# Two-layer transformer on one core: shared-expert weights loaded during the second attention, expert totals summed in PSUM by TensorE, and results finished for two chunks at once

## The reference

```python
scores = sigmoid(xf @ gate_w + bias)
top_scores, top_idx = top_k(scores, 2)           # weights of the two chosen experts
up = einsum('th,ehi->tei', xf, up_w) + up_b
eo = einsum('tei,eih->teh', gelu(up), down_w) + down_b
combined = einsum('teh,te->th', eo * 0.1, w)      # routed rows, two per token
shared = (gelu(xf @ sw_up + sb_up) @ sw_down + sb_down) * 0.1
out = shared + combined
out = out / (max(abs(out), axis=-1) + 1e-06)
return x + attention + out
```

## Time and profile before

| what | us |
|---|---|
| runs, median (lowest to highest, 3 runs) | 1303.87 (1302.80 to 1305.22) |
| profiled execution, its time | 1305.71 |
| profiled execution, span of the core | 1304.0 |
| mean granted TensorE clock, of full speed | 0.926 |
| TensorE busy | 1127.9 (86%) |
| VectorE busy | 971.5 (75%) |
| ScalarE busy | 740.4 (57%) |
| GpSimd busy | 509.9 (39%) |

### The profile page before, as it was taken

How to read it: one execution, slowest core, us unless ns; L and a number is a source line. 1 busy time by engine, 2 the same in 40 slices (tenths; PEclk the granted TensorE clock), 3 DMA queues, 4 the chain that set the end, 5 groups by cost and what they waited for, 6 DMA issues and landing times. The chain is left out here.

```text
span 1304.0 us, 22545 instructions
## 1 busy us (share of the span) xinstructions
PE 1127.9 (86%) x7455; PEld 619.1 (47%) x7458; DVE 971.5 (75%) x2126; ACT 740.4 (57%) x1143; POOL 509.9 (39%) x778
## 2 busy tenths in 40 slices
PE   4768879999999999999996755799999969999983
PEld 2436653444333434443433433444444438888862
DVE  8979978788888888888842533777777646777788
ACT  3657531666666656665664322166656557777762
POOL 6002220323233323332212526176666661566663
PEclk9889995999999999999987776599999989999997
DMA  4322970013121213120000121012222153678452
GB/s 130 97 79 68 129 85 18 26 38 126 34 75 50 91 35 99 38 94 27 2 2 1 54 76 44 23 48 64 58 64 63 38 178 110 189 235 241 152 130 65
DMA packets 94975, 103.51 MB, mean 79 GB/s; under 512 B 17217, under 2 KB 72838, under 8 KB 94864
## 3 DMA queue, kind: packets, MB, share of 16 engines
q1 hardware_dynamic: 88928, 93.09, 26.4%
q0 software_dynamic: 4992, 8.48, 1.9%
q10 hardware_dynamic: 944, 0.54, 0.2%
HBM read 64.67 MB, written 38.43 MB: 79 GB/s over the span
## 5 line engine op out<-in xcount | busy, mean ns | idle before, releaser
L1112 ACT ACTIVATE a_probs<-a_pst 128x1024 f32<-128x1024 f32 (+4 forms) x544 | 414.4, 813 | 284.5 <-PE a_pst L1060 284.0
L1136 DVE TENSOR_REDUCE a_tops<-a_ps 128x1 f32<-128x512 f32 (+9 forms) x624 | 341.4, 590 | 92.4 <-PE a_ps L1030 84.1
L976 POOL TENSOR_SCALAR_AFFINE_SELECT a_probs<-a_probs 128x256 f32<-128x256 f32 (+3 forms) x384 | 179.8, 480 | 387.3 <-ACT a_probs L1112 382.6
L1030 PE MATMUL a_ps<-kp,qp 96*128 96x512 bf16 (+9 forms) x1280 | 292.8, 307 | 0.8 <-DVE a_tops L1136 0.4
L1060 PE MATMUL a_pst<-qp,kp 99*128 99x512 bf16 (+4 forms) x1088 | 260.7, 332 | 22.6 <-DMA qp<-a_top_rows 18.9
L1079 PE MATMUL a_po<-a_probs,vh 128*32 128x512 f32 (+4 forms) x2176 | 233.1, 501 | 2.0 <-POOL a_probs L976 1.9
L1136 DVE TENSOR_REDUCE a_tops_lead<-a_ps 128x1 f32<-128x512 f32 x256 | 161.8, 683 | 5.7 <-PE a_ps L1030 5.4
L1027 PE MATMUL a_ps<-mask_s,identb 128*128 128x128 bf16 (+8 forms) x624 | 144.3, 234 | 7.0 <-PEq L1220 4.5
L1030 PEld LDWEIGHTS a_ps<-kp,qp 96*128 96x128 bf16 x1280 | 111.9, 101 | 79.1 <-DVE a_tops_lead L1136 15.3
L1060 PEld LDWEIGHTS a_pst<-qp,kp 99*128 99x128 bf16 (+1 forms) x1088 | 92.1, 100 | 120.1 <-ACT a_probs L1112 48.4
L1678 POOL DMA_INDIRECT chosen_rows<-e_slot_y,e_slot_x x92 | 93.4, 1015 | 87.9 <-DVE e_slot_y L1866 60.3
(11 more groups left out here) (269 smaller groups left out, 1715.7 us busy)
## 6 DMA issues: line engine op xcount, KB each, us to landing
e_slot_w<-weight_parts SPq DMA_DIRECT2D x23, 1024.0 KB
weight_parts<-a_cut SPq DMA_DIRECT2D x18, 512.0 KB, 3.1
qp<-q_parts SPq DMA_DIRECT2D x64, 96.0 KB
slot_rows<-empty_row SPq DMA_DIRECT2D x4, 1495.0 KB, 27.3
e_slot_x<-slot_rows SPq DMA_DIRECT2D x23, 260.0 KB, 5.4
a_raw<-in_wraw SPq DMA_DIRECT2D x18, 256.0 KB, 3.7
qp<-q_parts SPq DMA_DIRECT2D x64, 64.0 KB
q_parts<-o SPq DMA_DIRECT2D x24, 128.0 KB
```

The source lines that it names most:

```text
L976: pool.affine_select(out=seen, in_=seen, compare_op=ALU.is_ge, fill=0.0, base=m0, pattern=[[0, 2], [1, mw]], channel_multiplier=-1 if laye ...
L1030: last = pe.matmul(bank[:, i * room:i * room + w], sb["qp"][slot][0:KROWS, j, f["qt"] * P:(f["qt"] + 1) * P], sb["kp"][slot][0:KROWS, j // ...
L1112: act.activation(probs[local % RING][0:st["rows"], 2 * part:2 * part + 2, st["off"]:CHUNK], p_st[part][0:st["rows"], :, st["off"]:CHUNK], ...
L1136: dve.tensor_reduce(out, scores, AX.X, ALU.max).then_inc(s["banks_read"], 1)
```

## The change

Four things are changed.

1. The shared expert's weights and bias (`shared_w`, `shared_b`) get buffers that live through the whole program. Their three DMAs are issued by SP at the end of attention 1's list (`load_shared`) and no longer at the head of `experts`.
2. GpSimd's 16 adds of the totals are gone. The total of a chunk is now summed in a PSUM bank by TensorE: for chunks 2 to 7 the turned sums are written there (`turn_total`), for chunks 0 and 1 the kept rows in `e_acc` are multiplied by the identity, and then the two routed rows are added by two products with the identity as the stationary operand (`add_rows`, 128x512 in fp32). `e_acc` holds only two chunks, and ScalarE copies only those.
3. The banks `e_pt`, `e_pa`, `e_px`, `e_py` are used in turn, in the order `FINAL` of the chunks; `bank_free` is what TensorE waits for before it writes one again. `TURN_AT` and `ADD_AT` say at which step a turn or an add stands; the adds of the last three chunks stand behind the last step.
4. VectorE finishes two chunks at once: two reductions, three small instructions on 8 columns, eight result instructions. Results go to `big` (the whole input of the stage, no longer read by then), so there is no wait for a store. Two pair finishes stand at steps 121 and 124, two behind the last step. SP loads the routed rows in the order of `FINAL`.

```diff
+def load_shared(sp, io, sb, dram):
+    for i in range(2):
+        sp.wait_ge(sb["counts"]["experts"][f"cut_stored{i}"], START + 16 * CUTS // 2)
+    shared_in = sb["landed"]["shared"]
+    sp.dma_start(sb["shared_b"][:, :], io["wbias"][EXPERTS, :, :]).then_inc(shared_in[0], 16)
+    for c in range(2):
+        sp.dma_start(sb["shared_w"][:, 2 * c:2 * c + 2, :].rearrange("p a h -> p (a h)").bitcast(F32),
+                     dram["weights"][2 * EXPERTS + c, :, :]).then_inc(shared_in[c], 16)
...
+            if layer == 1:
+                load_shared(sp, io, sb, dram)
...
+        p_total = [p_t, p_a, p_x, p_y]
-        FINISH_AT = [HT * (JOBS - 2 + i // 2) + 2 * (i % 2) + 1 for i in range(4)]
-        LATE_FINISHED = len(FINISH_AT)
+        FINAL = [2, 3, 0, 4, 1, 5, 6, 7]
+        FINISH_AT = {HT * (JOBS - 1) + 1: 0, HT * JOBS: 1}
+        TURN_AT = {HT * (EARLY + n + SLOT_TILES + 2): EARLY + n for n in range(3)}
+        TURN_AT.update({HT * JOBS: 5, HT * JOBS + 2: 6, HT * (JOBS + 1): 7})
+        ADD_AT = {HT * (JOBS - 2) + 1: 0, HT * (JOBS - 2) + 3: 1, HT * (JOBS - 1) + 1: 2, HT * (JOBS - 1) + 3: 3,
+                  HT * JOBS + 1: 4}
...
-            for n in range(CHUNKS):
-                pool.wait_ge(chosen_in[n // 2], 2 * 16 * TOPK)
-                tiles = slice(n * CT, (n + 1) * CT)
-                pool.tensor_tensor(picked[0][:, tiles, :], picked[0][:, tiles, :], picked[1][:, tiles, :], ALU.add)\
-                    .then_inc(s["pairs_added"], 1)
-                pool.wait_ge(s["pairs_added"], START + n + 1)
-                pool.wait_ge(s["rows_done"], START + shared_job(n) + 1)
-                pool.tensor_tensor(acc[:, tiles, :], acc[:, tiles, :], picked[0][:, tiles, :], ALU.add)\
-                    .then_inc(s["totals_added"], 1)
...
+            def turn_total(n):
+                at, j = FINAL.index(n), shared_job(n)
+                pe.wait_ge(s["sums_read"], START + j + 1)
+                bank_free(at)
+                for t in range(CT):
+                    last = pe.matmul(p_total[at % 4][:, t * P:(t + 1) * P], sums[j % 2][:, t * P:(t + 1) * P],
+                                     sb["ident"][:, :], start=t == 0, stop=False, is_transpose=True,
+                                     skip_group_check=True)
+                last.then_inc(s["y_turned"], 1)
+
+            def bank_free(at):
+                if at == 0:
+                    pe.wait_ge(s["ot_copied"], START + CHUNKS)
+                elif at == 1:
+                    pe.wait_ge(s["x_added"], START + CHUNKS)
+                elif at == 2:
+                    pe.wait_ge(s["x_tail"], START + EARLY + SLOT_TILES)
+                elif at == 3:
+                    pe.wait_ge(s["rows_done"], START + EARLY + SLOT_TILES)
+                else:
+                    pe.wait_ge(s["res_ready"], START + CT * (at - 3))
+
+            def add_rows(at):
+                n = FINAL[at]
+                tiles = slice(n * CT, (n + 1) * CT)
+                whole = p_total[at % 4][:, :].rearrange("p (t e) -> p t e", e=E)
+                if n < EARLY:
+                    bank_free(at)
+                    pe.wait_ge(s["rows_done"], START + n + 1)
+                    pe.matmul(whole, sb["ident"][:, :], acc[:, tiles, :], start=True, stop=False, skip_group_check=True)
+                if at % 2 == 0:
+                    pe.wait_ge(chosen_in[at // 2], 2 * 16 * TOPK)
+                for i in range(TOPK):
+                    last = pe.matmul(whole, sb["ident"][:, :], picked[i][:, tiles, :], start=False, stop=i == TOPK - 1,
+                                     skip_group_check=True)
+                last.then_inc(s["totals_added"], 1)
...
-                if k == 0 and j >= 2:
+                if k == 0 and 2 <= j < 2 + EARLY + SLOT_TILES:
                     turn_y(j - 2)
+                if m in TURN_AT:
+                    turn_total(TURN_AT[m])
+                if m in ADD_AT:
+                    add_rows(ADD_AT[m])
...
             run(step)
+            for at in range(len(ADD_AT), CHUNKS):
+                add_rows(at)
...
+            def finish(pair):
+                step, base = s["res_steps"], RES * pair
+                total = [p_total[at % 4][:, :].rearrange("p (t e) -> p t e", e=E) for at in (2 * pair, 2 * pair + 1)]
+                for i in range(2):
+                    dve.wait_ge(s["totals_added"], START + 2 * pair + i + 1)
+                    dve.tensor_reduce(top[:, i * CT:(i + 1) * CT], total[i], AX.X, ALU.max, apply_absolute_value=True)\
+                        .then_inc(step, 1)
...
+                for i in range(2):
+                    n = FINAL[2 * pair + i]
+                    for t in range(CT):
+                        dve.scalar_tensor_tensor(res[:, n * CT + t, :], total[i][:, t, :], inv[:, i * CT + t:i * CT + t + 1],
+                                                 X[:, n * CT + t, :], ALU.mult, ALU.add).then_inc(s["res_ready"], 1)
```

More of the change, by code:

```diff
@@ L1574, in experts @@
         sums = [tmp(f"sums{i}", [P, CHUNK]) for i in range(2)]
[L1575 removed]
+        acc = tmp("acc", [P, EARLY * CT, E])
         o_t = tmp("o_t", [P, CHUNK])
[L1577 to L1578 removed]
+        top, inv = tmp("top", [P, 2 * CT]), tmp("inv", [P, 2 * CT])
         p_up = [bank(f"pup{i}") for i in range(UR)]
@@ L1818, in step @@
                     act.activation(o_t[:, :], p_t[:, :], ACT.Copy).then_inc(s["ot_copied"], 1)
-                if k == 0 and j >= 2 and shared_chunk(j - 2) is not None:
+                if k == 0 and 2 <= j < 2 + EARLY:
                     keep_rows(j - 2)
@@ L1905, in step @@
                 if m in FINISH_AT:
-                    finish(FINISH_AT.index(m))
+                    finish(FINISH_AT[m])
             stage_x(0)
             run(step)
-            for n in range(LATE_FINISHED, CHUNKS):
-                finish(n)
+            for pair in range(len(FINISH_AT), CHUNKS // 2):
+                finish(pair)
 def build(nc, io, out):
```

47 lines of the change are left out of this document (16 added, 31 removed).

## The result

The changed kernel takes 1290.66 us (median of 4 runs, 1289.20 to 1291.62), the kernel before, run beside it on the same chip, 1304.55 (1302.80 to 1306.50). The ratio is 0.9892, 95% interval 0.9874 to 0.9911: faster by 13.9 us, where 7.2 were forecast. The direction was right, the size too small by almost half.

A forecast was written before the change was run, and what follows sets the result against it. Bound by TensorE's own sum up to 1265, then by VectorE slowed beside GpSimd's adds, finally by VectorE's finishes. Start 0.6 plus end 6.6 gave 7.2 us off 1303.87: 1296.7, range 1293.8 to 1300.8.

The forecast's parts named there:

- 0.6 + 6.6 = 7.2 us: Whole forecast gain: 0.6 us at the experts' start plus 6.6 at the end, nothing elsewhere.
- recorded range: Forecast bounds for the changed kernel's time: 1293.8 us to 1300.8 us.
- start (to job 1): Head of experts' stage: early shared-weight load starts TensorE 0.55 us sooner; 0.6 taken as gain to job 1.
- the second of the two readings: Experts' start: VectorE stays tied to the ends of GpSimd's adds, gain between 0 and 1.4 us, a step.
- GpSimd's adds go: Late experts' stage: without 16 adds, VectorE subtractions return to 0.69 us; 4.65 us stall and slow clock vanish.
- TensorE's adds: Totals on TensorE: each fp32 identity product costs 0.86 us; 0.97 upper bound at full clock, 1.86 at the slow one.
- rival A: TensorE pays more: adds at 0.97 us plus small gaps; gain 4 to 5, about 1299.5 us; chance 0.14.
- Waits for routed rows and banks: From step 117: routed rows land and pair finishes free banks before TensorE needs them; no stall.
- Rival B: From step 117: late routed rows idle TensorE, which then runs at slow clock; about 1311.5 us; chance 0.04.
- the slack from step 117: First four routed-row loads landed by 1259.50, needed at 1262.6: 3.1 us of slack.
- The end: Last down to turn 1.17 us, pair finish 4.12, store tail 2.81; VectorE ends at 1294.6, not 1301.19: 6.6 saved.
- Rival D: More gain: start's step falls well (1.4 us), fewer small gaps at end; gain 9, about 1295 us; chance 0.08.

The follow-up runs named there:

- e1: Kernel before with 32 unused bytes per partition after the last kept buffer, moving every attention buffer by 32 bytes: 1297.35 us, ratio 0.995.
- e14: Changed kernel with 32 unused bytes ahead of the routed weights (e_slot_w), in the experts' stage alone: 1293.30 us, ratio 0.9906.
- e5: Kernel before with only the early load of the shared weights into kept buffers, totals and finishes as before: 1297.18 us, ratio 0.9948.
- e9: e8 with GpSimd's bias adds also spread over the first eight jobs (all but the first hunk): 1285.30 us, ratio 0.9848.
- e13: e9 with 32 unused bytes ahead of all the experts' temporaries: 1284.95 us, ratio 0.9839.
- e16: e9 with 96 unused bytes ahead of all the experts' temporaries: 1286.47 us, ratio 0.9845.
- e12: Kernel before with 32 unused bytes ahead of the routed weights (e_slot_w), in the experts' stage alone: 1303.71 us, ratio 0.9994.
- e15: Kernel before with 96 unused bytes ahead of the routed weights, in the experts' stage alone: 1310.52 us, ratio 1.0017, times widely spread.
- e17: Kernel before with 224 unused bytes ahead of the routed weights, in the experts' stage alone: 1302.52 us, ratio 0.9972.
- e18: Kernel before with 2016 unused bytes ahead of the routed weights, in the experts' stage alone: 1304.72 us, ratio 0.9988.
- e3: Kernel before with the attention's operands (v1, qp, kp, vh) moved by 32 bytes and the temporaries by 64: 1297.15 us, ratio 0.9951.
- e7: Changed kernel with 16 GpSimd adds put back on two buffers nobody else reads: 1301.33 us, ratio 0.9971.
- e4: Kernel before with only the attentions' temporaries moved by 32 bytes, operands where they were: 1299.61 us, ratio 0.9976.
- e10: Kernel before with 64 unused bytes after the last kept buffer: 1301.87 us, ratio 0.9994.
- e2: Changed kernel with 32 unused bytes, attention buffers placed as in the kernel before modulo 64: 1293.96 us, ratio 0.9923.
- e6: Changed kernel without the early load: shared weights loaded at the head of the experts' stage into the same kept buffers: 1289.06 us, ratio 0.9877.
- e11: Kernel before with 96 unused bytes after the last kept buffer: 1301.48 us, ratio 0.9971.
- e8: Changed kernel with the adds of chunks 5 and 6 placed ahead of the last turn: 1289.35 us, ratio 0.9895.

## Why the prediction was wrong, by its steps

The step that failed is a term that is not written down: the sum "0.6 + 6.6 = 7.2 us" put the place of the buffers, which the kept shared buffers move, at nothing without a reason, in the attentions and in the routed jobs alike. The runs showed 6.6 us there (e1) and 2.3 (e14). Eight other profiled kernels have the changed kernel's placement in the attentions (e5 to e9, e13, e14, e16), four others that of before (e12, e15, e17, e18), and the two groups keep apart: attention 0 and 1 together took 735.4 to 739.2 us in the changed kernel and its eight, and 741.6 to 746.3 in before and its four. The means are 7.0 us apart (737.3 and 744.3), so some 2.5 of the 9.5 us in the first table are the spread of single executions. The runs e1 and e3 make it a cause: 6.6 and 6.8 us by 32 bytes. The routed jobs' 2.2 us are the second part that was counted at nothing; e14 gives 2.3 for it. That the recorded range missed is due to these two; the two terms that were priced, 7.2 us, measured 6.5.

| term | predicted, us | measured in the profiles, us |
|---|---|---|
| start (to job 1) | 0.6 | 0.15 |
| routed jobs | 0 | 2.2 |
| end | 6.6 | 6.4 |
| experts' stage in all | 7.2 | 8.7 |
| attentions and what lies between | 0 | 8.4 (9.5 less 1.1); 6.6 in the medians of e1 |

*Start.* The first product came 0.45 us sooner on the stage's clock, near the 0.55; job 1 only 0.15. The ends of GpSimd's adds set when VectorE gets on, as the second of the two readings in the prediction had it. The Trainium skill (SBUF — State Buffer, Who interferes with whom) gives that reading: a lock for a whole instruction, so a step and not a rate. The traces agree: a cast takes 1.53 beside the adds and 0.43 in e9 without them, and an earlier start bought no earlier end. The 0.6 taken was the wrong choice of the two.

*GpSimd's adds go.* Right: subtractions 0.69 up to the end, no stall, clock 1.00. e7 gives the other side, 10.7 us for having them beside TensorE's adds.

*TensorE's adds.* 0.86 us, as taken from the one row of another stage; rival A falls: the range was open to a smaller gain by it, not to the larger one that came.

*Waits for routed rows and banks.* None; TensorE's only wait after job 1 is the 0.34 us before its last turn. Rival B did not occur, and the slack from step 117 held.

*The end.* Last down to turn 1.17 forecast, 1.18 measured; a pair 4.12 and 4.12; the tail 2.81 and 2.8. From job 29 on 6.4 in place of 6.6. The count of TensorE's end took 0.229 us for each product, from the shared jobs of before; they took 0.233 after, and for the 51 products from step 117 on that is 0.2 us (an estimate from these two paces), which fits the difference.

*Rival D* names 9 us, and the stage gained 8.7 by luck for it, but its reasons (a good step at the start, fewer gaps at the end) are not what happened.

**What stays open.** Why the last packet's wait depends on the address, and by which rule (e4 and e10 fit no simple one). Why the changed kernel loses only 3.3 us to the 32 bytes that give the old one 6.6 (e2). Whether a distance of 192 bytes is fast or in between, and why the shared jobs are slower than the routed ones at the same distance. The sum of the parts found, 6.6 by e1 and 8.7 in the experts' stage, is 15.3 us, 1.4 more than the medians' 13.9; nothing here says where the rest lies. Which of e9, e13 and e16 is best: their stages are 231.7, 230.6 and 231.9 us, their times 1285.30, 1284.95 and 1286.47, on different chips.

## What to carry to other kernels

Before a gain is credited to an edit, cut both traces at the stages' borders: time that moves in a stage the edit does not touch is placement, and an unused buffer of a few bytes in the old kernel tests it for the price of one run. Adding or removing any long-lived buffer moves all that lie behind it, so give it a range, here 9 us (6.6 and 2.3), and look at the addresses modulo 256. Where a DMA and a slow engine end at the same time, ask what holds the engine before hiding the DMA: the early load gave nothing, and moving GpSimd's bias adds off the same instants gave 3.9 us (+12.66 to +8.72).

## What the runs showed of the hardware that was not expected

- A product fp32r 128x512 follows the next after 0.228 us (0.229 to 0.230 in the shared jobs) where weights and moving operand lie a multiple of 256 bytes apart and after 0.232 to 0.233 at 32, 64, 128 or 224 bytes past it, at a granted clock of 1.00: 2.3 us over 23 jobs of 24 products. At 192 it was 0.230, in shared jobs alone.
- The wait from the last of 96 packets of 256 bytes, SBUF to SBUF, to the engine that reads them is 0.92 to 1.31 us at the median with the buffers' addresses; the time from issue to the first packet (1.40) and the transfer (0.50) are the same. Moving the buffers by 32 bytes is worth 6.6 us here.
- After the same 1.7 us wait TensorE went on at a granted clock of 1.00 in one execution and 0.73 in another, and 1.6 us were lost or not. Job 2 starts at about +20.2 in the traces of before, e1, e3 to e6, e11, e12, e14, e15, e18 and the changed kernel, and at +21.7 to +21.8 in those of e2, e7, e8, e10 and e17: a difference of that size between two single profiles is not an edit's.
- An fp32 product of 128x512 takes TensorE 0.86 us in two records, between fp32r products as in the first projection, and a bank that four transposes had filled (3.2 us before, for `e_px`) took it without a gap.
